# A sparse expert stage whose register loads are spread over its tiles, and an attention that completes its own last batch

## What is computed

```python
x = x + jnp.tanh(g_xattn[1]) * _L1_xattn_ref(_layernorm(x, axis=-1), ctx_1024, ctx_1024, ...)   # ends in a layernorm of its own
x = x + jnp.tanh(g_ffn[1]) * _L1_ffn_ref(_layernorm(x, axis=-1), L1_ffn_gate_w, L1_ffn_gate_up_w, L1_ffn_down_w)
...
top_k_probs, top_k_idx = jax.lax.top_k(router_probs, TOP_K)              # 8 experts, 2 for each row
gate_up = jnp.einsum('nd,edh->enh', x_flat, gate_up_w)
hidden = jax.nn.silu(gate_up[..., :F]) * gate_up[..., F:]                # F = 256
expert_out = jnp.einsum('enf,efd->end', hidden, down_w)
output = jnp.sum(sel * top_k_probs[:, :, None], axis=1)
```

## Time and profile before

| | us |
|---|---|
| median of 3 runs | 1545.75 (1542.09 to 1549.71) |
| the profiled execution | 1551.7 |
| its span, from the first to the last instruction | 1549.7 |
| the end of the attention's steps to the first matmul of the next layer | 552 to 671 of that span |
| busy on PE, DVE, ACT, POOL | 1285.8, 947.3, 717.8, 532.2 |

### The profile page before, as it was taken

One profiled execution on the slowest core, in us unless ns is written; L12 is line 12 of the kernel. 1 busy time (PEld: TensorE's weight loads), 2 busy tenths in 40 slices (PEclk: granted clock), 3 DMA queues, 4 the chain that ended last, 5 costly groups with the idle time before them and its releaser, 6 DMA issues. The chain is left out here.

```text
span 1549.7 us, 25211 instructions
## 1 busy us (share of the span) xinstructions
PE 1285.8 (83%) x8930; PEld 742.1 (48%) x8930; DVE 947.3 (61%) x2159; ACT 717.8 (46%) x1936; POOL 532.2 (34%) x625
## 2 busy tenths in 40 slices
PE   3799718889999958858996789898987968997998
PEld 2444316645555635544433456565654434443443
DVE  6466621265766753366664788888673855665764
ACT  3254503367666513443443565656663243453222
POOL 2310250445333534340001574747452220001443
PEclk8599959989999979876997999999997986998999
DMA  2455121151000013130000000000000001000000
GB/s 59 114 157 127 27 71 38 40 115 15 1 1 1 10 58 108 47 70 10 10 2 1 1 1 1 1 1 1 1 2 1 1 17 16 11 3 1 7 7 14
DMA packets 67134, 45.31 MB, mean 29 GB/s; under 512 B 17707, under 2 KB 60403, under 8 KB 67011
## 3 DMA queue, kind: packets, MB, share of 16 engines
q1 hardware_dynamic: 61155, 34.48, 8.7%
q0 software_dynamic: 4096, 8.40, 2.2%
q10 hardware_dynamic: 1760, 0.82, 0.3%
HBM read 24.91 MB, written 13.89 MB: 25 GB/s over the span
## 5 line engine op out<-in xcount | busy, mean ns | idle before, releaser
L3511 ACT ACTIVATE L2a_pr<-psum,L2a_negmax 128x512 f32<-128x512 f32 (+3 forms) x256 | 132.0, 530 | 95.0 <-DVE L2a_negmax L3637 40.2
L586 ACT ACTIVATE L1x_praw<-psum,L1x_negmax 128x154 f32<-128x154 f32 x256 | 95.9, 389 | 57.4 <-DVE L1x_negmax L710 57.4
L3376 PE MATMUL psum<-ident,L2a_pr 128*128 128x128 f32 x640 | 86.6, 280 | 20.3 <-DVE L2a_pT L3650 12.9
L320 POOL TENSOR_TENSOR L1x_pm<-L1x_praw,L1x_total 128x1024 f32<-128x1024 f32 x32 | 60.7, 1898 | 122.7 <-DVE L1x_total L716 104.0
L3376 PEld LDWEIGHTS psum<-ident,L2a_pr 128*128 128x128 f32 x640 | 72.4, 144 | 26.0 <-issue 23.7
L2049 POOL TENSOR_TENSOR L3f_scaled<-L3f_sg,L3f_wide 128x512 f32<-128x512 f32 (+1 forms) x44 | 55.8, 1273 | 66.8 <-ACT L3f_sg L2128 37.8
L1682 DVE TENSOR_REDUCE L3x_negmax<-psum 128x6 f32<-128x924 f32 (+1 forms) x48 | 47.7, 1011 | 46.7 <-PE psum L1220 37.4
L1682 DVE TENSOR_REDUCE L0x_negmax<-psum 128x6 f32<-128x924 f32 (+1 forms) x48 | 47.7, 1010 | 45.8 <-PE psum L1220 41.5
L3264 POOL TENSOR_TENSOR L2a_pr<-L2a_pr,L2a_total 128x768 f32<-128x768 f32 x32 | 48.7, 1520 | 69.9 <-DVE L2a_total L3666 69.6
L3261 POOL TENSOR_TENSOR L2a_pr<-L2a_pr,L2a_total 128x1024 f32<-128x1024 f32 x29 | 56.5, 1948 | 46.0 <-DVE L2a_total L3666 45.9
L710 DVE TENSOR_REDUCE L1x_negmax<-psum 128x4 f32<-128x616 f32 x64 | 50.8, 795 | 31.6 <-PE psum L391 28.3
(11 more groups left out here) (753 smaller groups left out, 3332.9 us busy)
## 6 DMA issues: line engine op xcount, KB each, us to landing
expert_arena<-in_L_ffn_w SPq DMA_DIRECT2D x16, 256.0 KB, 4.5
group_in<-zero SPq DMA_DIRECT2D x2, 1472.0 KB, 9.3
L1f_xs<-group_in SPq DMA_DIRECT2D x10, 256.0 KB, 3.9
group_out<-L1f_ys SPq DMA_DIRECT2D x10, 256.0 KB, 2.7
L1f_gu<-in_L_ffn_gate_up_w SPq DMA_DIRECT2D x8, 256.0 KB, 3.7
slots_in<-zero SPq DMA_DIRECT2D x1, 1280.0 KB, 9.2
L0f_xs<-slots_in SPq DMA_DIRECT2D x5, 256.0 KB, 4.3
resid<-in_x SPq DMA_DIRECT2D x4, 256.0 KB, 5.9
```

The lines of the kernel that those rows point to most:

```text
L320: nc.gpsimd.tensor_tensor(pm[:, n % 2].rearrange("p j t k -> p (j t) k"), praw[:, n % 3, :, :, 0:MAIN].rearrange("p j t k -> p (j t) k"), ...
L586: nc.scalar.activation(praw[:, n % 3, j, t, :], psum[:, 2 * u + j, x * CTX:(x + 1) * CTX], ACT.Exp, bias=negmax[:, n % 2, u, j, x:x + 1], ...
L3376: last = nc.tensor.transpose(psum[:, TURN + n // 4, n % 4 * P:(n % 4 + 1) * P], pr[:, m % RING, n * P:(n + 1) * P], core.ident[:])
L3511: ins = nc.scalar.activation(pr[:, i % RING, SEQ * j + lo:SEQ * j + hi], psum[:, bank + j, lo:hi], ACT.Exp, bias=negmax[:, i % RING, e:e + ...
```

## The change

Two things are moved. First, `experts` loads a range of tiles. Six numbers of group 0 are loaded at the end of the attention. In each step of a group the number for the tile five steps on is loaded right behind `up`, in steps 1 to 17. The first six numbers of group 1 are loaded in steps 17 to 22 of group 0. There are 46 loads as before, each now with a semaphore wait of its own (long fulfilled in the loop). Second, the last batch of the attention gets its parts 0 to 3 and its `root` in the attention's own block; the copy of that work at the head of the expert block, its square root on ACT and the buffers go away. With it the order at the head of the expert block changes: PE transposes the second half's rows and makes its logits ahead of step 0, ACT moves them out ahead of the first `turned`, and `best`, `ranks` and `place` each come one or two steps earlier.

```diff
@@ wide_attention, on PE, ACT and DVE
-                grouped.experts(pe, 0)
+                grouped.experts(pe, 0, 0, 6)
...
                 output(B - 1)
+                root(B - 1)
...
-                dve.wait_ge(s["yt_ps"], B)
-                nc.vector.tensor_tensor(core.last.rows, psum[:, IN, :].rearrange("p (t d) -> p t d", d=D), xn[:, (B - 1) % 3], ALU.add).then_inc(s["yr"], 1)
-                dve.wait_ge(s["yr"], B)
+                for part in range(4):
+                    finished(B - 1, part)
@@ Grouped
-    def experts(self, pe, k):
+    def experts(self, pe, k, x0, x1):
         pe.wait_ge(self.s["table"], k + 1)
-        for x in range(self.TILES):
+        for x in range(x0, x1):
             self.expert[k * self.TILES + x] = pe.value_load(self.of[0:1, k, x:x + 1])
@@ grouped_experts, on PE
                 pe.wait_ge(loaded, 16 * n_loads)
+                grouped.rowsT(pe, 2, xn[:, 0], ROUTE)
+                grouped.rowsT(pe, 3, xn[:, 1], Y[1])
                 turn(0)
+                grouped.logits(pe, 1, [xT[:, 0], xT[:, 1]], ROUTE)
                 for k in range(GROUPS):
                     if k:
-                        grouped.experts(pe, k)
                         turn(k * QUADS)
                     for x in range(STEPS):
                         i = k * TILES + x
                         if x < TILES:
                             up(i)
+                            if 0 < x and x + 5 < TILES:
+                                grouped.experts(pe, k, x + 5, x + 6)
+                        if k == 0 and 17 <= x < 23:
+                            grouped.experts(pe, 1, x - 17, x - 16)
...
-                        if k == 0 and x == 1:
-                            grouped.rowsT(pe, 2, xn[:, 0], ROUTE)
-                            grouped.rowsT(pe, 3, xn[:, 1], Y[1])
-                        if k == 0 and x == 2:
-                            grouped.logits(pe, 1, [xT[:, 0], xT[:, 1]], ROUTE)
-                        if k == 0 and x == 4:
+                        if k == 0 and x == 3:
                             pe.wait_ge(g["lg"], 2)
                             grouped.ranks(pe, 1, ROUTE)
@@ grouped_experts, on ACT
-                act.wait_ge(s["last_var"], 1)
-                nc.scalar.activation(last_sd[:], last_sd[:], ACT.Sqrt).then_inc(s["last_sd"], 1)
+                grouped.spread_root(act, 1)
+                nc.scalar.activation(sg[:, 0, 0:1], core.ident[:, 0:1], ACT.Silu)
+                grouped.rows_out(act, 2, xT[:, 0], ROUTE)
+                grouped.rows_out(act, 3, xT[:, 1], Y[1])
                 turned(0)
-                grouped.spread_root(act, 1)
-                nc.scalar.activation(warm[:], core.ident[:, 0:1], ACT.Silu)
...
@@ grouped_experts, on DVE (the last batch's statistics, normalization, sum and new statistics are taken out ahead of this)
...
                 grouped.spread(1)
                 for b in (2, 3):
                     grouped.front(dve, v, b, xn[:, b % 2])
...
+                        if k == 0 and x == 0:
+                            grouped.best(dve, v, 1, 0, ROUTE)
                         if k == 0 and x == 2:
-                            grouped.best(dve, v, 1, 0, ROUTE)
-                        if k == 0 and x == 3:
                             grouped.best(dve, v, 1, 1, ROUTE)
-                        if k == 0 and x == 5:
+                        if k == 0 and x == 4:
                             grouped.place(dve, v, 1, ROUTE)
```

More of the change, by code:

```diff
@@ L280, in wide_attention @@
         rows = got[:].rearrange("p (b t d) -> p b t d", b=2, d=D)
-        core.last = Last(core.x1[:, 0:QT, :], w["gamma"], w["beta"], gate)
         turned_rows = [xnT[:], xn[:, 1].rearrange("p t d -> p (t d)")]
@@ L812, in _ @@
                         finished(B - 2, (NS - 2, NS, NS + 1).index(n) + 1)
-                dve.wait_ge(s["yt_ps"], B)
-                nc.vector.tensor_tensor(core.last.rows, psum[:, IN, :].rearrange("p (t d) -> p t d", d=D), xn[:, (B - 1) % 3], ALU.add).then_inc(s["yr"], 1)
-                dve.wait_ge(s["yr"], B)
-class Last:
-    def __init__(self, rows, gamma, beta, gate):
-        self.rows, self.gamma, self.beta, self.gate = rows, gamma, beta, gate
+                for part in range(4):
+                    finished(B - 1, part)
 def add_rows(core, v, b, src, gate, new, base=None):
@@ L2859, in grouped_experts @@
     s = {n: nc.alloc_semaphore(f"{L}_{n}") for n in (
-        "vec", "th", "st_ps", "st", "up", "silu", "hid", "ht_ps", "ht", "down", "y", "summed", "last_var", "last_sd")}
+        "vec", "th", "st_ps", "st", "up", "silu", "hid", "ht_ps", "ht", "down", "y", "summed")}
     rows_in = [nc.alloc_semaphore(f"{L}_rows_in{q}") for q in range(GROUPS * QUADS)]
@@ L2888, in grouped_experts @@
         mv = sb("mv", [P, QT, 2])
-        last_sd = sb("last_sd", [P, QT])
-        warm = sb("warm", [P, 1])
         wt = core.slot_wt
-        last = core.last
         with nc.Block() as block:
@@ L3036, in _ @@
                             turned(k * QUADS + x // 4 + 1)
-                        if k == 0 and x == 1:
-                            grouped.rows_out(act, 2, xT[:, 0], ROUTE)
-                            grouped.rows_out(act, 3, xT[:, 1], Y[1])
                         if 0 <= x - 2 < TILES:
@@ L3075, in added @@
                         keep_rows(core, v, b, new, parts, mv)
-                for t in range(QT):
-                    v.step(nc.vector.bn_stats(parts[:, t, :], last.rows[:, t, :]))
-                v.done()
-                for t in range(QT):
-                    v.step(nc.vector.bn_aggr(mv[:, t, :], parts[:, t, :]))
-                v.done()
-                nc.vector.tensor_scalar(last_sd[:], mv[:, :, 1], LN_EPS, None, ALU.add).then_inc(s["last_var"], 1)
-                dve.wait_ge(s["last_sd"], 1)
-                v.step(nc.vector.reciprocal(last_sd[:], last_sd[:]))
-                v.done()
-                for t in range(QT):
-                    v.step(nc.vector.tensor_scalar(new[:, t, :], last.rows[:, t, :], mv[:, t, 0:1], last_sd[:, t:t + 1], ALU.subtract, ALU.mult))
-                v.done()
-                v.step(nc.vector.tensor_tensor(new[:], new[:], last.gamma[:].unsqueeze(1).to_broadcast([P, QT, D]), ALU.mult))
-                v.done()
-                v.step(nc.vector.tensor_tensor(new[:], new[:], last.beta[:].unsqueeze(1).to_broadcast([P, QT, D]), ALU.add))
-                v.done()
-                add_rows(core, v, B - 1, new[:].rearrange("p t d -> p (t d)"), last.gate, new)
-                keep_rows(core, v, B - 1, new, parts, mv)
                 grouped.spread(1)
```

## The result

| | before | changed |
|---|---|---|
| median | 1546.27 us (4 runs, 1542.09 to 1549.71) | 1536.98 us (4 runs, 1535.43 to 1537.14) |
| span of the profiled execution | 1549.7 | 1535.1 |

The ratio is 0.9932 with a 95% interval of 0.9906 to 0.9958: 9.3 us less by the medians, 6.5 to 14.5 by the interval. The forecast was 1533 and the range 1528 to 1541. The profiles differ by 14.6 us, but only a part of that is the change. To read it off I count from the first DVE instruction behind the barrier to the first matmul of the next layer, L1123 in the kernel before and L1115 in the changed one: 670.98 - 562.98 = 108.00 before, 658.97 - 561.45 = 97.52 after. The fence has the row of before; that of after stands under "The seam".

What follows compares the result with a forecast made beforehand. TensorE was taken as the bound in a group's steady part, POOL's DRAIN at the barrier. The terms 3.7 + 0 + 0 + 9.2 = 12.9 us gave a median of 1533 us, range 1528 to 1541.

Steps and rivals of the forecast that it cites:

- The barrier, 0: Barrier opening the expert block: fewer loads on PE and the moved chain gain 0, since POOL's DRAIN ends last.
- The front, 3.7: Head of group 0: first up 3 us later, but seventh up at 580.65 instead of 584.32, gain 3.7 us.
- A load in every tile, 0: Tiles of both groups: 40 register loads fit the sequencer's free 0.55 us per tile and cost 0 us.
- The seam, 8.6 + 3.4: Between the groups: 8.61 us of idle PE go, and a warm clock saves 3.4 more up to the seventh up.
- The gathers, 9.2 of slack: Group 1's second add: POOL's gathers of group 0 leave 9.2 us of slack, so 2.8 of 12.0 are lost.
- (a): Rival at group 1's gathers: they don't hold, or the wait is caught up; 15.7 us count, 1530; chance 0.13.
- (b): Rival in the tiles: loads cost 0.1 us a tile, 2.2 in group 0; gain 10.7 us, 1535; chance 0.10.
- (d): Rival in the tiles: each load holds the array by 0.3 us, eating 12 of 15.7; 1542; chance 0.10.
- (e): Rival in the tiles: loads wait for the array to finish, 0.8 us each; 16.3 us slower, 1562; chance 0.05.
- (c): Rival at group 0's head: low clock in the logits, or chain outlasting POOL's drain, removes the front's gain; 1539; chance 0.12.

Runs made afterwards that it cites:

- e3: Changed kernel with POOL's gathers of group 0's results two pairs deep instead of one; 1532.82 us, ratio 0.9905 to the kernel before.
- e12: Changed kernel with gathers two pairs deep and unread identity transposes around the barrier and in the wait ahead of the first turn; 1531.13 us, ratio 0.9896.
- e8: Changed kernel with three used register loads per tile, one for up and one for each down matmul; 1565.94 us, ratio 1.0134.
- e2: Changed kernel with each group's 23 register loads in one row again, only last batch and head order changed; 1546.41 us, ratio 0.9988.
- e4: Changed kernel with doubled loads that left 46 loads and only a short semaphore wait more in each step; 1534.23 us, ratio 0.9912.
- e7: Changed kernel with two used register loads per tile, one for up and one for down; 1547.08 us, ratio 1.0008.
- e6: Changed kernel with gathers two pairs deep and the second half's logits behind the first two ups; 1532.03 us, ratio 0.9901.
- e10: Changed kernel with unread identity transposes around the barrier and gathers two pairs deep; 1534.83 us, ratio 0.9927.
- e9: Changed kernel with unread identity transposes in PE's idle time around the barrier; 1534.59 us, ratio 0.9925.

## Why the prediction was right, and where not

**The barrier, 0: right.** In all fourteen profiles DVE starts 4.93 to 4.94 us behind POOL's last scatter, with 6 to 23 loads on PE, with and without the moved chain on DVE. The chain is hidden, by 0.8 us, and no scatter was stretched beside it (0.96 as in the earlier trace rows).

**The front, 3.7: mis-sized; it was 1.3,** just below the lower bound of 1.4 that I had given for a clock that stays low. The step that failed is the one that let the clock "rise on the way" in the logits and counted six tiles at 1.52 from there. The first up was on time to a tenth; from it to the seventh it took 11.85 us instead of 9.5. That this was the clock, and not DVE's `best` or the ranks, is shown by e3 and e12: with the changed kernel's front as it is and the clock at 1.00 from 5.4 on the term is 4.2 (21.34 - 17.10), with the same order at 1.00 all along 4.3. What settles the clock in a given execution is open: e3 and e8 have the changed kernel's front and rose at 5.4 and 5.5, as against 12.5 to 13.1 in the changed kernel, e2, e4 and e7.

**A load in every tile, 0: right, with less room than counted.** Tiles of 1.52 us (596.08 - 594.56) with a load in each. The load's price was right, 0.36 on the sequencer where the forecast had 0.38; the free time was counted too high, so that about 0.07 us were left by the estimate from e7 and e8, and not 0.17. The Trainium skill's floor of about 600 ns ("DMA: Bandwidth & Descriptors", "Latency and other measured facts") is not what a load lasts here (46 loads with a median of 302 ns).

**The seam, 8.6 + 3.4: right.** 8.6 and 2.8 were measured; the second lies within its 2.5 to 4.1 (ACT's copy behind the turn, a wait of 1.06, was not made up for by the first tiles).

**The gathers, 9.2 of slack: right, the best-founded number of the sum.** 12.9 us ahead at the seventh up of group 1, 2.4 given back in step 19; e3, e6 and e10 take the wait away by the gathers alone and win 2.4 to 2.5, counted from the seventh up.

By the trace the sum is 1.3 + 8.6 + 2.8 + 0.2 - 2.4 = 10.5 (the 0.2 lie in the tiles of group 0 behind the seventh) against 12.9, and the miss is the front's 2.4. Three readings in the forecast's working were off without moving the sum: from 571.1 the 8.2 us of the routing end at 579.3, not 579.9, and either lies ahead of the 580.2 of the tiles; the address work of `up` in the earlier trace rows ends at 600.03 (its instruction of 46 ns is the later one), which makes the sequencer's lead 0.46 us instead of 0.34; and 0.55 us of free time were more than the sequencer had. Of the rivals, (a) needs an end without the wait, which e3 shows is not what happened; (b), (d) and (e) fall with a tile of 1.52; (c) was half true: the front gained little, for the reason that it named first, but neither the chain nor POOL's drain had a part in it.

## What to carry to other kernels

When a row of short sequencer instructions stands between two full stretches of the array, deal it out, but count what the array's clock gives back afterwards and follow what else hangs on the stretch before: here a chain of gathers that hangs on group 0's end alone decided what the seam was worth, and its slack could be read to a few tenths from the trace before. Here the sequencer's free time held one load and not a second one with its address work: price the second one too, and all that comes with it. And a forecast for a stretch right behind a barrier wants two values, one for each level of the clock.

## What the runs showed of the hardware

- With PE idle ahead of the barrier the clock was at 0.50 some 2 us after its last matmul (in the kernel before that ended at 553.30, and the clock fell at about 555.0). With idle transposes in the gap it held through the barrier (1.19 us without a matmul) and then fell early in the logits behind a like wait of 1.19 us (e9); with that wait filled it held through the same logits (e12).
- After the barrier, with the logits ahead of the ups and no idle transposes, it rose at 12.5 to 13.1 us in four executions and at 5.4 and 5.5 in two, a difference of 3 us at the seventh up (20.03 and 17.10) for one and the same order of instructions.
- Register loads beside a full array mostly took about 300 ns (a median of 302 in the changed kernel), and up to 609 in single ones (e7). On the sequencer a load took 0.36 us up to the next instruction, and the address work of a register of its own 0.21; one more of both in a tile cost 0.50 to 0.56 us.
- POOL's DRAIN ended about 4.0 us after the last scatter's generation whatever else ran (560.5 - 556.5 in the changed kernel, 562.08 - 558.05 before).
